# Normalising every softmax tile on VectorE instead of every other one

## The chip, the cores and the metric

The kernel runs on one Trainium2 chip, on all 8 of its cores. Each core has a matmul engine (TensorE, PE in the profile, with PEld for its weight loads), VectorE (DVE), ScalarE (ACT), GpSimd (POOL) and SyncE (SP), and 16 DMA engines. All eight cores run the same program on different data and exchange nothing with one another. The metric is the device time in microseconds (us) of the slowest core. Less is better.

## The reference, cut to what matters

The whole computation is a layer norm, then an attention block and a mixture of experts on the same normalised input, both added to the input:

```python
xn = _layernorm(x, axis=-1)                       # x: (4, 2048, 2048)
x = x + attn(xn, Wqkv, bqkv, Wout, bout) + ffn(xn, gate, gate_up, down, alpha)

# attn: 16 heads of 128, 4 key and value groups
scores = jnp.einsum('bqhd,bkhd->bhqk', q, k) / HD
prob = jax.nn.softmax(scores, axis=-1)
out = jnp.einsum('bhqk,bkhd->bqhd', prob, v).reshape(b, s, D)
return out @ Wout + bout

# ffn: 32 experts, top 8 by softmax of xn @ gate.T; per expert silu(g) * u, then down
```

The change concerns one line of it, the softmax: its last step divides each row of exponentials by the row's sum.

## The kernel before

Core c takes one half (1024 rows) of the sequence of batch c // 2 as its own queries, and keys and values of all 2048 rows. The stages follow one another, with a barrier over PE, DVE and ACT between them: layer norm and transposes, the gate, the projections to q, k and v (L490), attention (here), the output projection (L686), the 32 experts (L828 and L764), and the last transposes with the store (L880, L890).

The order of the work is written out by hand. The Builder class keeps one list of instructions for each engine, and each engine runs its list strictly in order. An operation of VectorE or ScalarE also waits until the one before it on the same engine has finished. What depends on another engine waits for a count: `st` counts PE's batches, `sv` VectorE's operations, `ss` ScalarE's.

The attention stage works on 128 tiles, i = 0 to 127. Tile i is head h = i // 8 and query block q = i % 8: 128 queries against 2048 keys. The steps of one tile are:

- **Scores** (L562): four matmuls of 128x512 into `ps_a`, which is four banks and the only buffer for scores. So the scores of tile i wait until the exponential of tile i-1 has read `ps_a`.
- **Exponential** (L577) on ACT: 128x2048 from `ps_a` to `p_exp0` or `p_exp1` (f32), with the row sum in `ssum2`. Then a logarithm of the sum (L580).
- **Bias and reciprocal** (L583, L585) on DVE: 128x1 each. The bias is what the exponential of tile i+2 subtracts.
- **Norm**: `pn_sb = p_exp * rssum`, 128x2048, f32 to bf16. For even i it runs on DVE (L589), for odd i on ACT (L595).
- **Transposes** (L608) on PE: 16 of 128x128 into `ps_b`. Then a **copy** (L622) on DVE from `ps_b` to `pnT`.
- Once a head (8 tiles) is transposed, **PV** (L636): 32 matmuls of 128x512 into the two halves of `ps_d`, and two copies to `attn_o` on ACT (L645).

The order in which a turn of the loop hands these out is what decides who waits. In turn i, PE gets the scores of tile i, then (if i % 8 is 2 and i is 10 or more) PV of the head before, then the transposes of tile i-2. DVE gets the copy of tile i-2, then bias and reciprocal of tile i, and the norm if i is even. ACT gets the two PV copies where there are any, then the exponential and the logarithm of tile i, and the norm if i is odd. So of the 127 intervals from one exponential to the next, 15 hold a PV (those that end at i = 10, 18, ..., 122), and PV of the last head comes after the loop. An interval that begins at an even tile is called even to odd below, one that begins at an odd tile odd to even.

Of the kernel before, what the change touches and what calls it, by code (L numbers as in the profile page):

```python
# [7 lines left out]
AF = mybir.ActivationFunctionType  # L8
# [94 lines left out]
def build_program():  # L103
# [18 lines left out]
    def sb(name, shape, dtype, off):  # L122
        return nc.alloc_sbuf_tensor_at(name, shape, dtype, offset=MBASE + off).ap()
# [38 lines left out]
    ssum2 = [sm.get("ssum2a", 1), sm.get("ssum2b", 1)]  # L162
    lns2 = [sm.get("lns2a", 1), sm.get("lns2b", 1)]
    nmax2 = [sm.get("nmax2a", 1), sm.get("nmax2b", 1)]
    rssum = sm.get("rssum", 1)
# [64 lines left out]
    p_exp = [sb("p_exp0", [128, S], F32, DYN), sb("p_exp1", [128, S], F32, 65536)]  # L230
    pn_sb = [sb("pn_sb0", [128, S], BF16, 24576), sb("pn_sb1", [128, S], BF16, 61440)]
# [20 lines left out]
    B = Builder(nc)  # L252
# [222 lines left out]
    for jc in range(24):  # L475
# [7 lines left out]
        for tblk in tblks:  # L483
# [22 lines left out]
            if jc < 16:  # L506
# [4 lines left out]
                                 scale=1.0 / HD), "ss")  # L511
# [32 lines left out]
    ev_normC = [None] * 128  # L544
    ev_biasC = [None] * 128
    ev_tpC = {}
# [22 lines left out]
    def emit_softmax(i, ev_sc):  # L569
        qb2 = i % 2  # L570
        B.wait("scalar", "st", ev_sc)
        if i >= 2:
            B.wait("scalar", ev_normC[i - 2][0], ev_normC[i - 2][1])
            B.wait("scalar", "sv", ev_biasC[i - 2])
        else:
            B.wait("scalar", "sv", ev_nz)
        ev_expC[i] = B.op("scalar", lambda e, qb2=qb2: e.activation(  # L577
            p_exp[qb2][:], ps_a[:], AF.Exp, bias=nmax2[qb2][:],
            accum_out=ssum2[qb2][:]), "ss")
        ev_ln = B.op("scalar", lambda e, qb2=qb2: e.activation(  # L580
            lns2[qb2][:], ssum2[qb2][:], AF.Ln), "ss")
        B.wait("vector", "ss", ev_ln)
        ev_biasC[i] = B.op("vector", lambda e, qb2=qb2: e.tensor_tensor(  # L583
            nmax2[qb2][:], nmax2[qb2][:], lns2[qb2][:], ALU.subtract), "sv")
        ev_rc = B.op("vector", lambda e, qb2=qb2: e.reciprocal(rssum[:], ssum2[qb2][:]), "sv")  # L585
        if i % 2 == 0:
            if (i - 2, 1) in ev_tpC:
                B.wait("vector", ev_tpC[(i - 2, 1)][0], ev_tpC[(i - 2, 1)][1])
            ev_normC[i] = ("sv", B.op("vector", lambda e, qb2=qb2: e.tensor_scalar_mul(  # L589
                pn_sb[qb2][:], p_exp[qb2][:], rssum[:]), "sv"))  # L590
        else:
            B.wait("scalar", "sv", ev_rc)
            if (i - 2, 1) in ev_tpC:
                B.wait("scalar", ev_tpC[(i - 2, 1)][0], ev_tpC[(i - 2, 1)][1])
            ev_normC[i] = ("ss", B.op("scalar", lambda e, qb2=qb2: e.activation(  # L595
                pn_sb[qb2][:], p_exp[qb2][:], AF.Identity, scale=rssum[:]), "ss"))

    def emit_tp(i):
        h, q = divmod(i, 8)
# [54 lines left out]
    for i in range(128):  # L654
        ev_sc = emit_scores(i)
        if i >= 2:
            if i % 8 == 2 and i >= 10:
                emit_pv(i // 8 - 1)
            emit_tp(i - 2)
            ev_pv_vlast[0] = B.cnt["sv"]  # L660
        emit_softmax(i, ev_sc)
# [296 lines left out]
```

How the kernel before makes its waits and increments, by code:

```python
    def op(self, eng, fn, inc=None, n=1):  # L43
        auto = self.SELF_SEM.get(eng)
        if auto is not None:
            assert inc in (None, auto), (eng, inc)
            self.wait(eng, auto, self.cnt[auto])
            inc = auto
            n = 1
        if inc is None:
            self.streams[eng].append(lambda e, fn=fn: fn(e))
            return None
        self.cnt[inc] += n
        sem = self.sems[inc]
        self.streams[eng].append(
            lambda e, fn=fn, sem=sem, n=n: fn(e).then_inc(sem, n))
        return self.cnt[inc]
# [4 lines left out]
    def wait(self, eng, semname, val):  # L62
        if val is None or val <= 0:
            return
        self.streams[eng].append(
            lambda e, s=self.sems[semname], v=val: e.wait_ge(s, v))
```

## Time and profile before

| | us |
|---|---|
| median of 3 runs | 5631.75 |
| lowest and highest run | 5631.26 and 5634.69 |
| the profiled execution's own time | 5630.57 |
| span of its slowest core (core 0) | 5629.0 |
| spans of the 8 cores | 5609.8 to 5629.0 |

| engine, whole span of core 0 | busy us | share |
|---|---|---|
| PE | 5033.4 | 89% |
| DVE | 1639.2 | 29% |
| ACT | 875.2 | 16% |
| POOL | 258.4 | 5% |

The span runs from the core's first instruction to its last. The profiled execution's own time is 1.6 us above it. The rows further below are from core 0 where they don't say otherwise. An idle time in square brackets stands in front of the operation that ended it, with the operation that released it. The busy times are those of the whole program, of which attention is about an eighth, so they don't say what bounds that stage. A few per cent of core 0's matmul records are missing: where a batch of four scores shows x3, its first one is not in the trace and its start reads late.

### The profile page before, as it was taken

Reading aid. Unit: us, or ns where it says so; the run is one execution under the profiler, and the core shown is the slowest. Engines: PE = TensorE matmul, PEld = TensorE weight load, DVE = VectorE, ACT = ScalarE, POOL = GpSimd, SP = SyncE. Lnnn points to the kernel's source line nnn. Section 1 sums busy time; section 2 is a strip of 40 time slices with the busy share of each in tenths; the row PEclk is TensorE's granted clock in tenths of the full one; section 3 lists DMA queues with packets and bytes.
Section 4 is the critical chain, followed back from the end, with each engine's and each line's share of the span. In section 5 each row is a group of like instructions: output and inputs, shape, how many; then the busy total and the mean of one; then the engine's idle time right before and its main releaser. Section 6 shows DMA issues by size and latency. Waiting matters only on the chain.

```text
span 5629.0 us, 63025 instructions; the slowest of 8 cores (5609.8 to 5629.0 us)
## 1 busy us (share of the span) xinstructions
PE 5033.4 (89%) x23551; PEld 2390.1 (42%) x24008; DVE 1639.2 (29%) x2416; ACT 875.2 (16%) x1109; POOL 258.4 (5%) x493
## 2 busy tenths in 40 slices
PE   3588656669899999999999999999999999999995
PEld 2434433334444444444444444444444444444443
DVE  3300334330122333322222222333322222223333
ACT  4212666651000000000000000000000000000000
POOL 0000000000000000000000000000000000000000
PEclk9599788869999999999999999999999999999997
DMA  4241000005544434444444444434444444444333
GB/s 167 75 68 23 1 1 1 1 3 83 95 73 74 75 68 74 73 79 72 75 73 74 75 72 75 72 69 78 72 78 73 75 72 74 75 74 73 68 64 120
DMA packets 79879, 378.30 MB, mean 67 GB/s; under 512 B 9696, under 2 KB 10848, under 8 KB 65248
## 3 DMA queue, kind: packets, MB, share of 16 engines
q0 software_dynamic: 70416, 323.03, 32.5%
q1 hardware_dynamic: 9168, 51.21, 2.7%
q8 instruction: 201, 3.29, 0.2%
q14 instruction: 94, 0.77, 0.0%
HBM read 688.80 MB, written 8.39 MB: 124 GB/s over the span
## 4 chain that ended last, share of the span: by engine, by line
PE 85%; ACT 6%; DVE 3%; DMA 3%; issue 2%; DVEq 0%; ACTq 0%; SPq 0%; POOLq 0%
PE ps_a L828 47%; PE ps_d L764 23%; PE ps_a L490 4%; ACT p_exp L577 3%; PE ps_d L636 2%; PE ps_a L562 2%; PE ps_a L686 2%; ACT pn_sb L595 2%; PE ps_b L796 1%; PE ps_b L608 1%; DMA x_re<-x_own 1%; PE ps_b L394 1%; DVE pnT L622 1%; DMA wgubuf<-gu 1%; PE ps_b L353 1%
## 5 line engine op out<-in xcount | busy, mean ns | idle before, releaser
L828 PE MATMUL ps_a<-xn_own,wgubuf 128*128 128x512 bf16 x12044 | 2692.8, 384 | 26.8 <-DMA wgubuf<-gu 12.8
L828 PEld LDWEIGHTS ps_a<-xn_own,wgubuf 128*128 128x128 bf16 x12288 | 1212.0, 99 | 1517.6 <-issue 104.4
L764 PE MATMUL ps_d<-hstash,wdbuf 128*128 128x512 bf16 x6016 | 1330.8, 379 | 10.3
L851 DVE TENSOR_TENSOR sg_sb<-ps_a,sg_sb 128x512 f32<-128x512 f32 x384 | 265.7, 692 | 2407.3 <-PE ps_a L828 2407.3
L764 PEld LDWEIGHTS ps_d<-hstash,wdbuf 128*128 128x128 bf16 x6144 | 595.9, 97 | 741.1 <-issue 181.8
L774 DVE TENSOR_TENSOR ffn_acc<-ffn_acc,ps_d 128x512 f32<-128x512 f32 x1024 | 704.8, 688 | 605.2 <-PE ps_d L764 602.0
L841 ACT ACTIVATE sg_sb<-ps_a 128x512 f32<-128x512 f32 x384 | 229.2, 597 | 2262.7 <-PE ps_a L828 2262.7
L562 PE MATMUL ps_a<-k_sb,q_sb 128*128 128x512 bf16 x470 | 172.9, 502 | 251.6 <-ACT p_exp L577 163.9
L60 POOL DMA_DIRECT2D wgubuf<-gu x384 | 202.6, 528 | 2604.4 <-PE ps_a L828 2555.6
L856 DVE TENSOR_TENSOR hstash<-sg_sb,c_rep 128x512 bf16<-128x512 f32 x384 | 265.9, 693 | 42.3 <-DVE sg_sb L851 3.2
L806 ACT ACTIVATE c_rep<-ps_b 128x512 f32<-128x512 f32 x64 | 38.2, 597 | 1533.0 <-PE ps_b L796 1533.0
L622 DVE COPY pnT<-ps_b 128x2048 bf16<-128x2048 bf16 x128 | 156.7, 1225 | 286.1 <-PE ps_b L608 284.7
L608 PEld LDWEIGHTS ps_b<-ident_b,pn_sb 128*128 128x128 bf16 x2048 | 179.8, 125 | 53.2 <-issue 40.5
L608 PE MATMUL ps_b<-ident_b,pn_sb 128*128 128x128 bf16 x2048 | 192.5, 268 | 3.3 <-ACT pn_sb L595 1.8
L562 PEld LDWEIGHTS ps_a<-k_sb,q_sb 128*128 128x128 bf16 x512 | 48.0, 110 | 314.3 <-issue 298.1
L490 PE MATMUL ps_a<-xn_own,wjbuf 128*128 128x512 bf16 x752 | 168.7, 383 | 8.9 <-DMA wjbuf<-wqkv 7.7
L577 ACT ACTIVATE p_exp<-ps_a,nmax2b 128x2048 f32<-128x2048 f32 x64 | 125.9, 1967 | 105.4 <-PE ps_a L562 105.4
L595 ACT ACTIVATE pn_sb<-p_exp,rssum 128x2048 bf16<-128x2048 f32 x64 | 128.1, 2002 | 69.6 <-DVE rssum L585 62.9
L577 ACT ACTIVATE p_exp<-ps_a,nmax2a 128x2048 f32<-128x2048 f32 x64 | 125.9, 1967 | 12.1 <-PE ps_a L562 5.7
L353 PE MATMUL ps_b<-ident_b,xnbf 128*128 128x128 bf16 x256 | 32.6, 308 | 106.1 <-ACT xnbf L335 82.5
L636 PE MATMUL ps_d<-pnT,vt_sb 128*128 128x512 bf16 x501 | 120.1, 397 | 2.9 <-DVE pnT L622 2.1
L686 PE MATMUL ps_a<-attn_o,woutbuf 128*128 128x512 bf16 x502 | 112.8, 385 | 8.0 <-DMA woutbuf<-wout 7.5
(99 smaller groups left out, 1149.7 us busy)
## 6 DMA issues: line engine op xcount, KB each, us to landing
wgubuf<-gu POOLq DMA_DIRECT2D x384, 512.0 KB, 5.1
wdbuf<-down POOLq DMA_DIRECT2D x64, 1536.0 KB, 10.7
xtile<-x_own SPq DMA_DIRECT2D x16, 1024.0 KB, 5.6
xtile<-x_nbr SPq DMA_DIRECT2D x16, 1024.0 KB, 5.5
wjbuf<-wqkv POOLq DMA_DIRECT2D x24, 512.0 KB, 5.1
woutbuf<-wout POOLq DMA_DIRECT2D x16, 512.0 KB, 5.0
x_re<-x_own SPq DMA_DIRECT2D x8, 1024.0 KB, 7.2
o<-out_sb SPq DMA_DIRECT2D x8, 1024.0 KB, 4.8
```

Source lines behind the costliest of these rows:

```text
L490: ins = e.matmul(ps_a[:, bank * 512:(bank + 1) * 512], wjbuf[jc % 2][:, dc * 128:(dc + 1) * 128], xn_mv(dc, tblk), start=(dc == 0), stop=( ...
L562: ins = e.matmul(ps_a[:, kb * 512:(kb + 1) * 512], q_sb[:, h * TOWN + q * 128: h * TOWN + q * 128 + 128], k_sb[:, g * S + kb * 512: g * S ...
L577: ev_expC[i] = B.op("scalar", lambda e, qb2=qb2: e.activation(p_exp[qb2][:], ps_a[:], AF.Exp, bias=nmax2[qb2][:], accum_out=ssum2[qb2][:]) ...
L595: ev_normC[i] = ("ss", B.op("scalar", lambda e, qb2=qb2: e.activation(pn_sb[qb2][:], p_exp[qb2][:], AF.Identity, scale=rssum[:]), "ss"))
L608: ins = e.matmul(ps_b[:, k * 1024 + j * 128: k * 1024 + (j + 1) * 128], pn_sb[qb2][:, kc * 128:(kc + 1) * 128], ident_b[:], is_transpose=True,
L636: ins = e.matmul(pv_ps, vt_sb[:, (g * 16 + kc) * 128:(g * 16 + kc) * 128 + 128], pnT[:, kc * TOWN + qb * 512: kc * TOWN + qb * 512 + 512], ...
L764: ins = e_.matmul(ps_d[:, slot * 512:(slot + 1) * 512], wdbuf[gh % 3][:, (dc % 8) * 768 + icc * 128: (dc % 8) * 768 + icc * 128 + 128], hs ...
L774: e_.tensor_tensor(ffn_acc[:, dc * TOWN + tb * 512: dc * TOWN + tb * 512 + 512], ffn_acc[:, dc * TOWN + tb * 512: dc * TOWN + tb * 512 + 512],
L828: ins = e_.matmul(ps_a[:, bank * 512:(bank + 1) * 512], wgubuf[bufi][:, dc * 128:(dc + 1) * 128], xn_own[:, dc * TOWN + tb * 512: dc * TOW ...
L841: ev_silu[(e, ip, tb)] = B.op("scalar", lambda e_, tb=tb: e_.activation(sg_sb[:, tb * 512:(tb + 1) * 512], ps_a[:, tb * 512:(tb + 1) * 512 ...
L851: ev_h1[(e, ip, tb)] = B.op("vector", lambda e_, tb=tb: e_.tensor_tensor(sg_sb[:, tb * 512:(tb + 1) * 512], ps_a[:, (2 + tb) * 512:(3 + tb ...
L856: e_.tensor_tensor(hstash[e2 % 2][:, ip * TOWN + tb * 512: ip * TOWN + tb * 512 + 512], sg_sb[:, tb * 512:(tb + 1) * 512], c_rep[e2 % 2][: ...
```

## The change

The norm of odd tiles moves from ACT to DVE, where the norm of even tiles already is. It is the same formula, with the same operands and the other pair of buffers. The wait for the transposes of tile i-2 (they read the same `pn_sb` buffer) moves with it, and the wait of ACT for the reciprocal goes. The event that PE waits for before the transposes of odd tiles is now one of VectorE's.

```diff
-        ev_rc = B.op("vector", lambda e, qb2=qb2: e.reciprocal(rssum[:], ssum2[qb2][:]), "sv")
-        if i % 2 == 0:
-            if (i - 2, 1) in ev_tpC:
-                B.wait("vector", ev_tpC[(i - 2, 1)][0], ev_tpC[(i - 2, 1)][1])
-            ev_normC[i] = ("sv", B.op("vector", lambda e, qb2=qb2: e.tensor_scalar_mul(
-                pn_sb[qb2][:], p_exp[qb2][:], rssum[:]), "sv"))
-        else:
-            B.wait("scalar", "sv", ev_rc)
-            if (i - 2, 1) in ev_tpC:
-                B.wait("scalar", ev_tpC[(i - 2, 1)][0], ev_tpC[(i - 2, 1)][1])
-            ev_normC[i] = ("ss", B.op("scalar", lambda e, qb2=qb2: e.activation(
-                pn_sb[qb2][:], p_exp[qb2][:], AF.Identity, scale=rssum[:]), "ss"))
+        B.op("vector", lambda e, qb2=qb2: e.reciprocal(rssum[:], ssum2[qb2][:]))
+        if (i - 2, 1) in ev_tpC:
+            B.wait("vector", ev_tpC[(i - 2, 1)][0], ev_tpC[(i - 2, 1)][1])
+        ev_normC[i] = ("sv", B.op("vector", lambda e, qb2=qb2: e.tensor_scalar_mul(
+            pn_sb[qb2][:], p_exp[qb2][:], rssum[:]), "sv"))
```

VectorE in the middle of a head, two tiles before the change. `pn_sb_139` and `p_exp_137` are the buffers of even tiles, `pn_sb_140` and `p_exp_138` those of odd ones.

```order
L622 COPY pnT<-ps_b 128x16x128
L583 TENSOR_TENSOR nmax2a<-nmax2a,lns2a 128x1
L585 RECIPROCAL rssum<-ssum2a 128x1
L589 TENSOR_SCALAR pn_sb_139<-p_exp_137,rssum 128x2048
L622 COPY pnT<-ps_b 128x16x128
L583 TENSOR_TENSOR nmax2b<-nmax2b,lns2b 128x1
L585 RECIPROCAL rssum<-ssum2b 128x1
```

The same place with the change, where the lines behind it have moved up by seven.

```order
L615 COPY pnT<-ps_b 128x16x128
L583 TENSOR_TENSOR nmax2a<-nmax2a,lns2a 128x1
L585 RECIPROCAL rssum<-ssum2a 128x1
L588 TENSOR_SCALAR pn_sb_139<-p_exp_137,rssum 128x2048
L615 COPY pnT<-ps_b 128x16x128
L583 TENSOR_TENSOR nmax2b<-nmax2b,lns2b 128x1
L585 RECIPROCAL rssum<-ssum2b 128x1
L588 TENSOR_SCALAR pn_sb_140<-p_exp_138,rssum 128x2048
```

A norm now also stands between the reciprocal of an odd tile and the next copy. ScalarE at the same place and around a PV, before the change:

```order
L577 ACTIVATE p_exp_138,ssum2b<-ps_a,nmax2b 128x2048
L580 ACTIVATE lns2b<-ssum2b 128x1
L595 ACTIVATE pn_sb_140<-p_exp_138,rssum 128x2048
L645 ACTIVATE attn_o<-ps_d 128x512 x2
L577 ACTIVATE p_exp_137,ssum2a<-ps_a,nmax2a 128x2048
L580 ACTIVATE lns2a<-ssum2a 128x1
L577 ACTIVATE p_exp_138,ssum2b<-ps_a,nmax2b 128x2048
L580 ACTIVATE lns2b<-ssum2b 128x1
L595 ACTIVATE pn_sb_140<-p_exp_138,rssum 128x2048
L577 ACTIVATE p_exp_137,ssum2a<-ps_a,nmax2a 128x2048
```

ScalarE there with the change:

```order
L577 ACTIVATE p_exp_138,ssum2b<-ps_a,nmax2b 128x2048
L580 ACTIVATE lns2b<-ssum2b 128x1
L638 ACTIVATE attn_o<-ps_d 128x512 x2
L577 ACTIVATE p_exp_137,ssum2a<-ps_a,nmax2a 128x2048
L580 ACTIVATE lns2a<-ssum2a 128x1
L577 ACTIVATE p_exp_138,ssum2b<-ps_a,nmax2b 128x2048
L580 ACTIVATE lns2b<-ssum2b 128x1
L577 ACTIVATE p_exp_137,ssum2a<-ps_a,nmax2a 128x2048
```

Between the logarithm of an odd tile and the next exponential nothing is left on ACT but the PV copies, once a head. PE's order is the same in both kernels, and so are all DMAs.

## Rows read from the trace of the kernel before

**Rows 1.** Spans and mean granted TensorE clock of the cores.

```profile
core 0: 5629.0 us, clock 0.938
```

**Rows 2.** Busy us (instructions) of PE, PEld, DVE, ACT, POOL; PEclk; DMA; by stretch.

```profile
543.60:1256.00 712.40, 455.66 (x2999) 277.76 (x3053) 280.69 (x450) 435.39 (x478) 0.00 (x0) 0.78 0.00 1
1400.00:5600.00 4200.00, 4094.95 (x18244) 1839.94 (x18613) 1247.91 (x1797) 265.07 (x444) 232.17 (x440) 0.98 0.41 75
```

**Rows 3.** Groups by line: busy us, mean ns | idle before, releasers.

```profile
L562 PE MATMUL ps_a<-k_sb,q_sb 128*128 128x512 bf16 x470 | 172.9, 502 | 251.6 <-ACT p_exp L577 163.9 <-ACT lns2a L580 60.5 <-ACT lns2b L580 24.7
...
L622 DVE COPY pnT<-ps_b 128x2048 bf16<-128x2048 bf16 x128 | 156.7, 1225 | 286.1 <-PE ps_b L608 284.7 <-DVE pn_sb L589 0.3
L595 ACT ACTIVATE pn_sb<-p_exp,rssum 128x2048 bf16<-128x2048 f32 x64 | 128.1, 2002 | 69.6 <-DVE rssum L585 62.9 <-PE ps_a L562 6.7
...
L589 DVE TENSOR_SCALAR pn_sb<-p_exp,rssum 128x2048 bf16<-128x2048 f32 x64 | 82.3, 1287 | 7.3 <-DVE rssum L585 0.7
...
L890 DVE TENSOR_TENSOR out_sb<-ps_a,x_re 128x2048 f32<-128x2048 f32 x8 | 18.3, 2292 | 64.5 <-DMA x_re<-x_own 64.5
```

**Rows 4.** One line, L577: duration ns min/median/max, first and last start.

```profile
L577 ACT ACTIVATE p_exp<-ps_a,nmax2a x64: 1967/1967/1967, 545.7 to 1237.4; 128x2048 f32<-128x2048 f32 x64
...
L577 ACT ACTIVATE p_exp<-ps_a,nmax2b x64: 1967/1967/1968, 550.0 to 1241.5; 128x2048 f32<-128x2048 f32 x64
```

**Rows 5.** Timeline, one pair of tiles: start us, us, operation, [idle before <-releaser].

```profile
708.50 1.97 ACT L577 ACTIVATE p_exp<-ps_a,nmax2a 128x2048 f32<-128x2048 f32 x1
...
710.71 1.86 PE L562 MATMUL ps_a<-k_sb,q_sb 128*128 128x512 bf16 x4 [3.51 <-ACT p_exp L577]
...
712.37 1.90 PE L608 MATMUL ps_b<-ident_b,pn_sb 128*128 128x128 bf16 x16
...
712.84 1.97 ACT L577 ACTIVATE p_exp<-ps_a,nmax2b 128x2048 f32<-128x2048 f32 x1 [1.98 <-PE ps_a L562]
...
715.04 1.02 PE L562 MATMUL ps_a<-k_sb,q_sb 128*128 128x512 bf16 x4 [0.77 <-ACT p_exp L577]
...
716.40 2.00 ACT L595 ACTIVATE pn_sb<-p_exp,rssum 128x2048 bf16<-128x2048 f32 x1 [1.21 <-DVE rssum L585]
...
718.50 1.97 ACT L577 ACTIVATE p_exp<-ps_a,nmax2a 128x2048 f32<-128x2048 f32 x1
```

**Rows 6.** Timeline around a PV.

```profile
722.62 1.97 ACT L577 ACTIVATE p_exp<-ps_a,nmax2b 128x2048 f32<-128x2048 f32 x1 [1.77 <-PE ps_a L562]
...
725.82 7.07 PE L636 MATMUL ps_d<-pnT,vt_sb 128*128 128x512 bf16 x31
...
733.04 0.60 ACT L645 ACTIVATE attn_o<-ps_d 128x512 bf16<-128x512 f32 x1 [2.86 <-PE ps_d L636]
733.73 1.97 ACT L577 ACTIVATE p_exp<-ps_a,nmax2a 128x2048 f32<-128x2048 f32 x1
```

**Rows 7.** Timeline, the tiles right behind that PV.

```profile
735.93 1.02 PE L562 MATMUL ps_a<-k_sb,q_sb 128*128 128x512 bf16 x4 [2.15 <-ACT p_exp L577]
736.25 0.16 DVE L583 TENSOR_TENSOR nmax2a<-nmax2a,lns2a 128x1 f32<-128x1 f32 x1 [1.00 <-ACT lns2a L580]
...
736.79 1.29 DVE L589 TENSOR_SCALAR pn_sb<-p_exp,rssum 128x2048 bf16<-128x2048 f32 x1
736.79 1.06 PE L608 MATMUL ps_b<-ident_b,pn_sb 128*128 128x128 bf16 x16
737.22 1.97 ACT L577 ACTIVATE p_exp<-ps_a,nmax2b 128x2048 f32<-128x2048 f32 x1 [1.14 <-PE ps_a L562]
738.18 1.22 DVE L622 COPY pnT<-ps_b 128x2048 bf16<-128x2048 bf16 x1
...
739.42 1.02 PE L562 MATMUL ps_a<-k_sb,q_sb 128*128 128x512 bf16 x4 [1.57 <-ACT p_exp L577]
```

**Rows 8.** Stretches of that timeline, columns as in rows 2.

```profile
738.00:739.40 1.40, 0.00 (x0) 0.01 (x1) 1.30 (x2) 1.31 (x3) 0.00 (x0) 1.00 0.00 0
...
744.91:748.20 3.29, 3.19 (x19) 2.10 (x18) 1.61 (x3) 1.54 (x1) 0.00 (x0) 0.50 0.00 0
```

## The prediction

> **What bounds the kernel now.** I read the spans first [rows 1]: core 0 is the slowest, and the profiled time is 1.6 us above its span. Then the stages [rows 2]. From 1400 to 5600 us, the experts, PE is busy 4095 of 4200 us at a granted clock of 0.98. The change touches nothing there. In attention, 543.6 to 1256 us, no engine is full: of 712 us PE is busy 456, ACT 435, DVE 281, and PE's clock is 0.78 on average. An unfilled stage like this is bound by a loop of waits, so I went to the groups and then to the timeline. The groups say that PE sat idle 251.6 us before the scores, nearly all of it until ACT had done an exponential or the logarithm just behind it, and that the odd norm (L595) costs ACT 64 x 2002 ns, after another 69.6 us of idling, mostly for DVE's reciprocal [rows 3].
>
> The whole loop runs from exponential to exponential. The first starts at 545.7 and the last at 1241.5 us [rows 4]: 695.8 us for 127 intervals, 15 of them with a PV.
>
> One pair of tiles shows the rhythm [rows 5]. Even to odd: exponential at 708.50, the scores of the next tile released by it at 710.71 (2.21 later), done 1.86 later at 712.57, next exponential 0.27 behind them at 712.84. That is 4.34 us, and only ACT to PE to ACT is in it. Odd to even: 712.84 to 718.50, 5.66 us. Here the scores start at 715.04 and end at 716.06, so the exponential could start at 716.33. But ACT's list has the norm first. It starts only at 716.40, after 1.21 us of waiting for the reciprocal, and ends at 718.40. So the norm holds the loop up for 718.50 - 716.33 = 2.17 us, and PE stands idle meanwhile: the next burst shows the result of it, since the scores at 710.71 had an idle 3.51 us in front of them, took 1.86 us and not 1.02, and the transposes behind them 1.90 us.
>
> **The clock is the second half of the effect.** At the low of its two levels (1.2 GHz, granted 0.50) PE needs 1.86 us for a batch of scores and about 1.90 for the 16 transposes; at the high one (2.4 GHz, granted 1.00) 1.02 and 1.06 [rows 5, 7, 8]. Behind the PV there is a stretch where PE had been busy for 7 us [rows 6] and the idle stretches were shorter: 2.15 us, then 1.57 us. There both score batches took 1.02 us and the clock stayed at 1.00 through the idle from 738.00 to 739.40. The interval 733.73 to 737.22 is 3.49 us [rows 6, 7]. That is the 4.34 of above less 0.84 for the faster scores. The clock fell again before the burst at 744.91 (0.50) [rows 8].
>
> The Trainium skill ("TensorE: Matmul & The Clock Gate", section "HAM oscillation") says that a PE which waits too long between short bursts starts each of them throttled. By that rule, as by my sum, removing the long wait returns the clock; the trace agrees.
>
> **The change, part by part.**
>
> 1. *The norm of odd tiles leaves ACT.* 64 x 2.00 us go. Of these 15 lie beside a PV: from 722.62 to 733.73 us the exponential waits for the PV matmuls (7.07 us from 725.82) and the copy at 733.04 that drains them [rows 6], and 11.11 us stay 11.11. In the other odd intervals what is late next is the scores, at 3.49 us if the clock is up or 4.34 if it is not. One norm lies behind the last exponential.
>
> 2. *The norm of odd tiles comes to DVE.* The even one takes 1287 ns [rows 3]. The odd one I take at the same, since type, shape and operation are the same. Its bounds are 1.29 and the 2.29 of a DVE operation of 128x2048 f32 with two tensor inputs [rows 3]. Does DVE keep up? An even tile's work there runs from 736.25 (bias) over the norm at 736.79 to the end of the copy at 739.40 [rows 7]: 3.15 us, with 0.1 to the next, 3.25. Each tile now has that, against an interval of 3.49. So DVE is a quarter of a microsecond short of being the bound. What is queued behind the odd norm is the copy of the tile before. It waits anyway for transposes that end 1.06 us behind the scores: at 739.42 + 1.02 + 1.06 = 741.5 us by rows 7, when a norm begun at 740.28 (bias 0.54 before it, as at 736.25) would end at 741.57. So the copy is 0.1 to 0.2 us later than before, ends near 742.9, and the next bias is wanted at 740.71 + 2.52 = 743.23. Nobody on the loop waits for it. Cost: nothing, and below zero it can't be, since the only gain of this part is a shorter norm (2.00 - 1.29 = 0.7 us) before the last transposes.
>
> 3. *The waits.* ACT's wait for the reciprocal goes (part of the 2.17). The exponential of tile i+2 now waits for DVE's norm of tile i; that ends 4.35 us after the exponential (738.08 against 733.73) and is wanted two intervals on, at 6.98. Hidden. PE's transposes of an odd tile wait for a norm that ends in front of the next scores' end. Hidden.
>
> 4. *The clock.* With the norm gone PE's longest idle in the loop is that of rows 7, about 1.4 to 1.6 us, in both kinds of intervals, and 2.15 us once behind each PV. Bounds: every interval at 3.49, or every one at 4.34. I take 3.49 for all but the first four, in which PE has few transposes and starts low: 4 x 0.85 = 3.4 us. Because the 2.15 us behind a PV is the stretch with the least work, I allow one interval at 4.34 in 6 of the 15 heads: 5.1 us (0 to 15).
>
> **Sum.** 112 intervals x 3.49 = 390.9; + 3.4 + 5.1; + 15 x 11.11 = 166.7; together 566.1 us in place of 695.8: 129.7 less. With 0.7 at the end 130.4 less. 5630.57 - 130.4 = 5500.2. The median of the runs was 1.2 us above the profiled execution, so 5501 us. All cores run the same loop, so the slowest falls as core 0 does.
>
> **Rivals.**
>
> *A, the clock stays low between PVs.* Then 112 x 4.34 + 166.7 = 652.8, 43 us less: 5588 us. For it: PE has work for 2.1 of 3.49 us only, and long parts of the stage now run low (0.78 on average). Against it: at the low level PE would be working 1.86 + 1.90 of 4.34 us, which is more than in the pairs of rows 5, where the clock came back during one such burst.
>
> *B, the clock goes up and down.* Half of the intervals at 4.34: 56 x 4.34 + 56 x 3.49 + 166.7 = 605.2, 91 less: 5540 us. Against it: two idle stretches of this size in a row (rows 7) did not bring the clock down. The Trainium skill (same page, "A second HAM failure mode: psum-queue depth-cycling") describes just this, a PE that idles briefly but often between groups and whose clock swings. The rows speak for the high level so far, but only for two or three intervals in a row, never for seven.
>
> *C, the odd norm is slower on DVE than the even one.* At 2.29 us DVE's two tiles take 3.25 + 4.25 = 7.5 us against 6.98: 56 x 0.52 = 29 us more than forecast, 5530 us. Against it: same shape, same types, only another buffer. The Trainium skill ("VectorE: DVE Perf Modes", "Mode 2×_2P") gives an f32 operation with one tensor input in SBUF its doubled rate by operand and memory, whichever buffer it is; by that C falls, and no row shows the odd norm.
>
> *D, slower than before.* DVE becomes the bound by contention: norms and copies now fill 2.51 of its 3.25 us a tile, always beside an exponential that writes the same memory. If that stretches them, the interval is 0.74 + 2.51 f. The average interval without a PV was (695.8 - 166.7) / 112 = 4.72, so it decides from f = 1.6. At f = 2 it is 5.76 x 112 + 166.7 = 812, 116 more: 5747 us. Against it: the norm at 736.79 lies for most of its time beside the exponential at 737.22, and the mean of all 64 is 1287 ns too.
>
> *E, nothing gained*, because the exponential waits for something else at the same time: 5632. Against it: rows 5 have the scores ready 2.4 us early.
>
> **How the numbers follow.** Forecast 0.80, A 0.04, B 0.07, C 0.06, D 0.02, E 0.01. A difference under 0.2% (11 us) can't be told from none here. Faster takes the forecast, A, B and C: 0.97; same 0.01; slower 0.02. The forecast alone spans 5489 (no interval low, 8.5 less, and a few us for the clock in the experts' stage) to 5518 (15 heads with one or two low intervals each). To leave no more than 2 in 10 out I take in C and B: 5488 to 5541.
>
> **What would show it.** The first and the last exponential 566 us apart; odd to even equal to even to odd, 3.49 us each, in the middle of a head; 11.1 around a PV; all 128 norms at 1287 ns; a granted clock in the attention stage above 0.95 and the idle before the scores about 1.5 us a tile; ACT's only idle until the scores. The copy should start directly behind the norm, and bias be released by the logarithm. I am wrong if many score batches still take 1.86 us (A, B), if bias waits for the copy of DVE (C, D), or if the experts' stage changes its length by more than a few us.

## The result, and the profile after

| | kernel before | changed kernel |
|---|---|---|
| median of the comparison on record | 6241.73 us (10 runs) | 5683.35 us (8 runs) |
| lowest | 5624.18 us | 5495.42 us |
| ratio to the kernel before | 1 | 0.9766, 95% interval 0.9747 to 0.9785 |
| the same in the later comparison (e9) | 1 | 0.9745, 95% interval 0.9694 to 0.9797 |

In five of the eight runs of the changed kernel the cores of one die had a lower granted clock and took longer (5632 to 6435 us), and the ratio leaves such runs out, as it does six of the ten runs of the kernel before (6126 to 6562 us). The other three runs of the changed kernel took 5495.42, 5499.28 and 5501.25 us. The forecast was 5501 us. The median over all eight, 5683.35 us, lies above its range of 5488 to 5541.

The spans of the first profile show both kinds of cores side by side.

```profile
core 0: 5493.0 us, clock 0.958
...
core 4: 6172.4 us, clock 0.846
```

The stretches, with the columns of [rows 2]. First core 4 of that profile in the experts' stage:

```profile
1400.00:5600.00 4200.00, 4172.54 (x16162) 1732.94 (x16161) 1077.11 (x1562) 232.84 (x390) 205.74 (x390) 0.84 0.35 63
...
3000.00:3400.00 400.00, 397.16 (x1481) 162.25 (x1480) 104.36 (x152) 20.30 (x34) 17.82 (x34) 0.80 0.34 61
```

And core 0 of the same profile at the same time:

```profile
3000.00:3400.00 400.00, 395.01 (x1759) 176.74 (x1794) 122.07 (x177) 25.08 (x42) 22.26 (x42) 0.99 0.41 72
```

Then core 0 of the second profile of the changed kernel (e9), attention and experts:

```profile
543.60:1131.00 587.40, 376.76 (x3088) 227.88 (x3088) 364.26 (x516) 308.66 (x417) 0.00 (x0) 0.95 0.00 1
1400.00:5400.00 4000.00, 3967.07 (x17939) 1764.43 (x17938) 1206.63 (x1750) 254.36 (x426) 223.78 (x424) 0.99 0.42 72
```

Against [rows 2]: the stretch cut out for attention is 587 us long where it was 712, DVE's work in it is up from 281 to 364 us and ACT's down from 435 to 309, and PE's clock is 0.95 in place of 0.78. In the experts' stage core 0 has the clock it had before. Core 4 of the first profile has 0.84, and 0.80 in the middle, where it gets through 1481 matmuls in 400 us and core 0 through 1759.

The groups, answering to [rows 3], of the second profile:

```profile
L588 DVE TENSOR_SCALAR pn_sb<-p_exp,rssum 128x2048 bf16<-128x2048 f32 x128 | 164.7, 1287 | 15.0 <-PE ps_a L562 1.1 <-PE ps_b L601 0.4 <-DVE rssum L585 0.4
L615 DVE COPY pnT<-ps_b 128x2048 bf16<-128x2048 bf16 x128 | 156.7, 1225 | 130.6 <-PE ps_b L601 119.9 <-DVE pn_sb L588 0.5
...
L562 PE MATMUL ps_a<-k_sb,q_sb 128*128 128x512 bf16 x512 | 138.7, 395 | 202.7 <-ACT p_exp L577 201.6 <-DVE vt_sb L539 1.1
```

All 128 norms take 1287 ns on average. PE's idle before the scores is 201.6 us for 127 intervals, 1.59 us each. The loop, answering to [rows 4]:

```profile
L577 ACT ACTIVATE p_exp<-ps_a,nmax2a x64: 1967/1968/1971, 549.0 to 1109.1; 128x2048 f32<-128x2048 f32 x64
...
L577 ACT ACTIVATE p_exp<-ps_a,nmax2b x64: 1967/1967/1969, 553.3 to 1112.6; 128x2048 f32<-128x2048 f32 x64
```

From 549.0 to 1112.6 us it is 563.6 us in place of 695.8; in the first profile it was 567.2 (547.0 to 1114.1). Over the eight cores the mean loop went from 696.0 (690.7 to 703.0) to 565.7 us (563.6 to 568.4) in the second profile. The span fell by 133.5 us from 5629.0 to 5495.5: 132.2 in the loop, 3.3 us were lost before it and 4.6 won behind it.

By kind of interval, on core 0: the 64 even-to-odd ones went from 4.00 to 3.56 us on average, 28 us together; the 48 odd-to-even ones without a PV from 5.54 to 3.56, 95 us; the 15 with a PV, which are all odd to even, from 11.60 to 10.98, 9 us. No even-to-odd interval ever had a norm of ACT in it, so their 28 us are the clock's.

A PV and the tiles behind it, in the same profile:

```profile
690.09 1.97 ACT L577 ACTIVATE p_exp<-ps_a,nmax2b 128x2048 f32<-128x2048 f32 x1 [1.14 <-PE ps_a L562]
...
693.15 7.07 PE L629 MATMUL ps_d<-pnT,vt_sb 128*128 128x512 bf16 x32
...
701.06 1.97 ACT L577 ACTIVATE p_exp<-ps_a,nmax2a 128x2048 f32<-128x2048 f32 x1
...
704.55 1.97 ACT L577 ACTIVATE p_exp<-ps_a,nmax2b 128x2048 f32<-128x2048 f32 x1 [1.14 <-PE ps_a L562]
705.51 1.22 DVE L615 COPY pnT<-ps_b 128x2048 bf16<-128x2048 bf16 x1
...
706.75 1.02 PE L562 MATMUL ps_a<-k_sb,q_sb 128*128 128x512 bf16 x4 [1.57 <-ACT p_exp L577]
707.07 0.16 DVE L583 TENSOR_TENSOR nmax2b<-nmax2b,lns2b 128x1 f32<-128x1 f32 x1 [0.34 <-ACT lns2b L580]
...
707.61 1.29 DVE L588 TENSOR_SCALAR pn_sb<-p_exp,rssum 128x2048 bf16<-128x2048 f32 x1
...
708.04 1.97 ACT L577 ACTIVATE p_exp<-ps_a,nmax2a 128x2048 f32<-128x2048 f32 x1 [1.14 <-PE ps_a L562]
```

Read it against [rows 5] and [rows 6]. 690.09 to 701.06 is 10.97 us, with the PV in it. The interval from the odd tile at 704.55 to the even one at 708.04 is 3.49 us, where it was 5.66. The exponential waits for the scores and for nothing else, the scores take 1.02 us, and bias waits 0.34 us for the logarithm and not for the copy.

### The profile page after: what moved, and what is told of

It reads as the page before. It is cut to its first block, busy times and chain, and to the rows that moved or that the text cites. A ratio compares the mean times of both kernels' runs of the same rounds, so it can differ in the third digit from the quotient of the medians.

```text
span 6172.4 us, 63418 instructions; the slowest of 8 cores (5483.8 to 6172.4 us)
## 1 busy us (share of the span) xinstructions
PE 5656.5 (92%) x24008; PEld 2503.3 (41%) x24008; DVE 1720.4 (28%) x2480; ACT 747.2 (12%) x1045; POOL 258.3 (4%) x493
## 4 chain that ended last, share of the span: by engine, by line
PE 89%; ACT 5%; DMA 3%; DVE 2%; issue 1%; ACTq 0%; DVEq 0%; SPq 0%; POOLq 0%
PE ps_a L821 51%; PE ps_d L757 25%; ACT p_exp L577 4%; PE ps_a L490 3%; PE ps_a L562 2%; PE ps_a L679 2%; PE ps_d L629 2%; PE ps_b L789 1%; DMA x_re<-x_own 1%; PE ps_b L394 1%; DMA wgubuf<-gu 1%; PE ps_b L353 1%; PE ps_d L378 0%; DMA xtile<-x_own 0%; DMA xtile<-x_nbr 0%
## 5 line engine op out<-in xcount | busy, mean ns | idle before, releaser
L821 PE MATMUL ps_a<-xn_own,wgubuf 128*128 128x512 bf16 x12288 | 3144.0, 428 | 11.8 <-DMA wgubuf<-gu 11.8
L821 PEld LDWEIGHTS ps_a<-xn_own,wgubuf 128*128 128x128 bf16 x12288 | 1313.4, 107 | 1858.2 <-issue 1545.0
L757 PE MATMUL ps_d<-hstash,wdbuf 128*128 128x512 bf16 x6144 | 1566.0, 426 | 0.6
L757 PEld LDWEIGHTS ps_d<-hstash,wdbuf 128*128 128x128 bf16 x6144 | 654.1, 107 | 907.2 <-issue 802.3
L562 PE MATMUL ps_a<-k_sb,q_sb 128*128 128x512 bf16 x512 | 141.8, 402 | 199.0 <-ACT p_exp L577 197.9
L588 DVE TENSOR_SCALAR pn_sb<-p_exp,rssum 128x2048 bf16<-128x2048 f32 x128 | 164.6, 1286 | 15.0 <-PE ps_a L562 1.5
L601 PEld LDWEIGHTS ps_b<-ident_b,pn_sb 128*128 128x128 bf16 x2048 | 138.0, 104 | 38.9 <-issue 14.7
L601 PE MATMUL ps_b<-ident_b,pn_sb 128*128 128x128 bf16 x2048 | 149.4, 231 | 4.2 <-DVE pnT L615 4.1
L577 ACT ACTIVATE p_exp<-ps_a,nmax2b 128x2048 f32<-128x2048 f32 x64 | 125.9, 1967 | 77.9 <-PE ps_a L562 68.5
L577 ACT ACTIVATE p_exp<-ps_a,nmax2a 128x2048 f32<-128x2048 f32 x64 | 125.9, 1967 | 66.7 <-PE ps_a L562 57.0
L789 PE MATMUL ps_b<-combineT,selbuf 32*128 32x512 f32 x128 | 88.2, 775 | 34.6 <-ACT c_rep L799 30.5
```

The costliest lines, as they stand in the source:

```text
L562: ins = e.matmul(ps_a[:, kb * 512:(kb + 1) * 512], q_sb[:, h * TOWN + q * 128: h * TOWN + q * 128 + 128], k_sb[:, g * S + kb * 512: g * S ...
L601: ins = e.matmul(ps_b[:, k * 1024 + j * 128: k * 1024 + (j + 1) * 128], pn_sb[qb2][:, kc * 128:(kc + 1) * 128], ident_b[:], is_transpose=True,
L757: ins = e_.matmul(ps_d[:, slot * 512:(slot + 1) * 512], wdbuf[gh % 3][:, (dc % 8) * 768 + icc * 128: (dc % 8) * 768 + icc * 128 + 128], hs ...
L821: ins = e_.matmul(ps_a[:, bank * 512:(bank + 1) * 512], wgubuf[bufi][:, dc * 128:(dc + 1) * 128], xn_own[:, dc * TOWN + tb * 512: dc * TOW ...
```

## The experiments

Times of loops are those of core 0. "Before" in a ratio is always the kernel before on the same chip. The matmuls that e2, e7 and e11 add write to a free half of `ps_d` and nobody reads them. The expectations of e2, e3 and e11 count 56 pairs of intervals without a PV. There are 64 even to odd and 48 odd to even, which makes their loops 644, 623 and 634 us in place of 658, 615 and 625.

**e1, all norms on ACT.**

```diff
-        if i % 2 == 0:
+        if False:
```

> The reverse of the change: the norm of even tiles goes to ACT too, so that all 128 are there. My theory (a norm in ACT's list holds the next exponential up until its end, whatever else is ready): all 112 intervals without a PV become like the odd-to-even ones of the kernel before. From exponential to exponential: 2.35 us to the end of the logarithm, reciprocal ended at 2.95, norm from about 3.15 to 5.15, next exponential at 5.25; with a late copy on DVE up to 5.67. So the loop takes 112 x 5.25 to 5.67 + 15 x 11.0 = 753 to 800 us in place of 696, and the kernel 5690 to 5735 us. Rival 1 (the change gained by the clock alone): PE's idle in even intervals gets longer, at most 4.34 us an interval, so no more than 5632 us. Rival 2 (the norm's own shorter duration on DVE is what counts, 0.7 us each): 64 x 0.7 = 46 us more, 5677 us, with intervals of about 5.

Measured: ratio 1.0141 (1.0112 to 1.017), median of all 4 runs 5708.26 us, loop 768.3 us. A stretch of its timeline:

```profile
702.62 1.97 ACT L577 ACTIVATE p_exp<-ps_a,nmax2b 128x2048 f32<-128x2048 f32 x1
...
704.83 1.86 PE L562 MATMUL ps_a<-k_sb,q_sb 128*128 128x512 bf16 x4 [2.17 <-ACT p_exp L577]
...
705.78 2.00 ACT L595 ACTIVATE pn_sb<-p_exp,rssum 128x2048 bf16<-128x2048 f32 x1 [0.80 <-DVE rssum L585]
...
707.87 1.97 ACT L577 ACTIVATE p_exp<-ps_a,nmax2a 128x2048 f32<-128x2048 f32 x1
```

The scores are ready at 706.69 even at the low clock, and the exponential comes at 707.87, behind the norm: 5.25 us, as expected, and the same number for most intervals of either kind. So a norm on ACT in front of the exponential sets the interval, though the scores are ready. Both rivals had smaller numbers (5632 and 5677 us).

**e2, the kernel before with PE kept busy.**

```diff
+        if i >= 11 and q != 2 and i % 2 == 1:   # in front of the scores
+            6 matmuls 128x512 into ps_d[:, 0:512]
```

> The kernel before, with 6 more matmuls of 128x512 in front of the scores of odd tiles (from the second head on, not behind a PV), whose results nobody uses: they fill part of the 3.5 us in which PE idles there and change nobody's order. It measures the clock's part alone. My theory: the clock stays at its high level, even to odd becomes 3.49 us, odd to even stays at 5.25 us because of the norm on ACT, so the loop takes 56 x 8.74 + 15 x 10.97 + about 4 = 658 us in place of 696 and the kernel about 5594 us (5587 to 5604): the clock is worth about 40 of the 130 us, the wait 90. Rival 1 (the gain was the clock's): the loop comes down most of the way to 566 us, and the kernel to 5520 or less. Rival 2 (the clock is only a by-product and costs nothing in this kernel): 5632 us.

Measured: ratio 0.9948 (0.9924 to 0.9972), median 5597.65 us, loop 666.6 us, granted clock in the loop 0.90:

```profile
543.80:1210.40 666.60, 479.97 (x3347) 271.78 (x3348) 275.71 (x443) 431.31 (x475) 0.00 (x0) 0.90 0.00 1
```

29 us less than 695.8, without any change to who waits for whom, and 23 of them in the even-to-odd intervals (from 4.00 to 3.64 us). The mean over the eight cores went from 696.0 to 664.0. The clock didn't stay up throughout: if it had, the corrected sum of 644 us makes its part 52 us. Odd to even stays at 5.25 us in 27 of 48 intervals. So the clock alone is worth 29 us as measured, 52 by this estimate, and what is left from 644 to 564, about 80 of the 132, needs the norm out of the way.

**e3, the odd norm late on ACT.**

```diff
+        flush()     # behind exponential and logarithm of tile i: norm of tile i-1, if odd
-            ev_normC[i] = ("ss", B.op("scalar", ... pn_sb[qb2], p_exp[qb2], scale=rssum))
+            pend.append((i, ev_rc))   # emitted by the next flush, with scale=rssum1
```

> The kernel before, with the odd norm still on ACT but behind the exponential and logarithm of the next tile, and a reciprocal buffer of its own. It separates where the norm stands from which engine does it. My theory: odd to even falls to 3.49 us as with the change; even to odd now holds exponential, logarithm and the norm, 2.35 + 0.1 + 2.0 + 0.1 = 4.54 us. A pair takes 8.03 us against 8.9 to 10 before and 6.98 with the change: loop 56 x 8.03 + 15 x 11.0 = 615 us, kernel about 5550 us (5540 to 5565). Rival (only taking the work from ACT helps, since ACT is the bound): 5632 us.

Measured: ratio 0.9997 (0.9985 to 1.0009), median 5627.70 us where 5550 was expected, loop 688.8 us. Even to odd took 4.65 us, odd to even 4.21 on average, around a PV 12.6. One pair:

```profile
701.51 1.97 ACT L578 ACTIVATE p_exp<-ps_a,nmax2a 128x2048 f32<-128x2048 f32 x1 [1.74 <-DVE rssum L587]
...
703.71 1.02 PE L563 MATMUL ps_a<-k_sb,q_sb 128*128 128x512 bf16 x4 [1.57 <-ACT p_exp L578]
703.96 2.00 ACT L605 ACTIVATE pn_sb<-p_exp,rssum 128x2048 bf16<-128x2048 f32 x1
...
706.16 1.97 ACT L578 ACTIVATE p_exp<-ps_a,nmax2b 128x2048 f32<-128x2048 f32 x1 [0.20 <-ACT pn_sb L605]
706.21 1.05 PE L618 MATMUL ps_b<-ident_b,pn_sb 128*128 128x128 bf16 x16 [1.48 <-ACT pn_sb L605]
...
708.36 1.87 PE L563 MATMUL ps_a<-k_sb,q_sb 128*128 128x512 bf16 x4 [1.10 <-ACT p_exp L578]
...
710.49 1.97 ACT L578 ACTIVATE p_exp<-ps_a,nmax2a 128x2048 f32<-128x2048 f32 x1 [1.98 <-PE ps_a L563]
```

The scores for the exponential at 706.16 were ready at 704.73; it waited for the late norm. And PE, with the transposes of the odd tile next in its list, now idles 1.48 us for the same norm. The scores at 708.36 run at the low clock. The idle had moved, and hardly shrunk.

**e11, the same with PE kept busy** (5 matmuls of 128x512 in front of the transposes of odd tiles).

```diff
+            emit_keep(i)        # 5 matmuls, odd i only
             emit_tp(i - 2)
```

> The kernel with the odd norm late on ACT, and 5 more matmuls (results unused) in front of the transposes of odd tiles, where PE waits 1.5 us for that norm. It took 4.65 + 4.21 us a pair and 12.6 us around a PV where I had expected 4.54, 3.49 and 11. Theory: half of the scores ran at the low clock, because the late norm moved PE's idle from in front of the scores to in front of the transposes and hardly made it less. With the clock held up a pair takes 4.65 + 3.49 and a PV interval about 11: loop 56 x 8.14 + 165 + 4 = 625 us, kernel 5560 us (5550 to 5575). Rival (the place of the norm brings nothing, on whatever clock): 5620 us.

Measured: ratio 0.9874 (0.9786 to 0.9962), fastest run 5569.26 us, loop 636.1 us at a clock of 0.96. The pair takes 4.65 + 3.58, a PV interval 11.1. So e3's missing gain was the clock's: 688.8 - 636.1 = 53 us. The corrected sum for e11 was 634 us. At nearly the same clock (0.96), e11 against the changed kernel is 636 to 564, and 70 of these 72 us lie in the 64 even-to-odd intervals: 4.65 us on average in place of 3.56, because exponential, logarithm and norm of ACT now fill the interval.

**e4, the PV copies behind the exponential.**

```diff
         emit_softmax(i, ev_sc)
+        if i % 8 == 2 and i >= 10:
+            emit_pvout(i // 8 - 1)     # was part of emit_pv, ahead of emit_softmax
```

> The changed kernel, with ACT's two PV copies behind the exponential of their turn in place of in front of it. My theory: with the norm gone the largest hold-up left in ACT's list is this one. Exponential i starts 3.49 us behind the one before it, beside the PV matmuls. Then PE is the bound: scores end at 3.22, PV 7.07 later at 10.29, transposes at 11.35, scores of tile i+1 at 12.4, exponential i+1 at 12.65 us, where it is 10.97 + 3.49 = 14.46 now. That is 1.8 us x 15 = 27 us less, and the 2.15 us idle behind a PV goes, and with it the low clock there, up to 9 us: kernel 5460 to 5475 us. Rival (DVE, which is 0.24 us a tile short of being the bound, can't catch up with the copy that PV delays, and gives the gain back): 5495 to 5500 us, with bias waiting for the copy in most of the tiles behind a PV.

Measured: fastest of six runs 5454.11 us, no ratio on record. In the profile cores 0 to 3 span 5442.8 to 5453.3 us, where those of the changed kernel's first profile span 5483.8 to 5497.3. Loop 524.0 us, clock 0.99. The two intervals around a PV are 3.49 + 8.66 = 12.15 us in place of 14.46, better than the 12.65 expected, and the low clock behind a PV is gone too. The rival's sign is there and costs nothing:

```profile
652.31 1.22 DVE L615 COPY pnT<-ps_b 128x2048 bf16<-128x2048 bf16 x1 [7.28 <-PE ps_b L601]
...
653.63 0.16 DVE L583 TENSOR_TENSOR nmax2a<-nmax2a,lns2a 128x1 f32<-128x1 f32 x1
...
656.33 1.97 ACT L577 ACTIVATE p_exp<-ps_a,nmax2a 128x2048 f32<-128x2048 f32 x1 [1.14 <-PE ps_a L562]
```

Bias starts right behind the copy, so DVE is behind, yet the exponential is 3.49 us behind the one at 652.84.

**e5, PV spread over the turns.** This is the version that beats both kernels. The two PV copies also move behind the exponential, as in e4.

```diff
         emit_tp(i - 2)
-        if i % 8 == 2 and i >= 10: emit_pv(i // 8 - 1)      # 32 matmuls, ahead of emit_tp
+        j = i - 6                                           # 4 matmuls a turn
+        if j >= 0: emit_pv_part(j // 8, (j % 8) // 4, j % 4)
...
-        if h >= 1 and q == 0: B.wait("vector", "st", ev_pvmm.get((h - 1, 1)))
+        if h >= 1 and q % 4 == 0: B.wait("vector", "st", ev_pvmm[(h - 1, q // 4)])
```

> The changed kernel, with the 32 PV matmuls of a head no longer in one block but four at a time behind the transposes of each turn (first half of the queries from tile 4 of the head on, second half from tile 0 of the next). My theory: with the norm on DVE what is left of the loop is exponential, scores, exponential, 3.49 us, in which PE is idle for 1.3 to 1.4 us. Four PV matmuls take 7.07 / 8 = 0.9 us and fit. So every one of the 127 intervals is 3.49 us, there are none of 11, and PE's clock never falls in the loop: 127 x 3.49 + 4 = 447 us in place of 567, kernel about 5375 us (5365 to 5395). Rival 1: DVE, at 3.25 us a tile, has no PV pause any more in which to catch up, and the PV copies of ACT come on top; the interval settles above 3.6 us and the kernel above 5390. Rival 2: nothing is gained against the block, since PE is the bound: about 5450 us.

Measured: ratio 0.9543 (0.9523 to 0.9564), median 5374.67 us, loop 446.4 us.

```profile
702.89 1.97 ACT L577 ACTIVATE p_exp<-ps_a,nmax2b 128x2048 f32<-128x2048 f32 x1 [1.14 <-PE ps_a L562]
703.36 1.03 PE L631 MATMUL ps_d<-pnT,vt_sb 128*128 128x512 bf16 x4
...
705.09 1.02 PE L562 MATMUL ps_a<-k_sb,q_sb 128*128 128x512 bf16 x4 [0.71 <-ACT p_exp L577]
705.33 0.60 ACT L642 ACTIVATE attn_o<-ps_d 128x512 bf16<-128x512 f32 x1
...
706.38 1.97 ACT L577 ACTIVATE p_exp<-ps_a,nmax2a 128x2048 f32<-128x2048 f32 x1 [0.45 <-PE ps_a L562]
```

PE idles 0.71 us before the scores, the PV copy fits into ACT's idle, and 3.49 us stay 3.49. Against e4, which has the late copies already, spreading alone took the loop from 524.0 to 446.4 us.

**e6, the same with the norm as before** (even on DVE, odd on ACT).

```diff
-            pn_sb[qb2][:], p_exp[qb2][:], rssum[:]), "sv"))     # all tiles on vector
+        (the branch on i % 2 of the kernel before)
```

> The same spread PV, but with the kernel before's norm: even tiles on DVE, odd ones on ACT. Here the clock can't be what differs, since PE gets 3.0 us of work in every interval. My theory: even to odd 3.49, odd to even 5.25 us (norm from 3.15 to 5.15 behind the exponential), both at the high clock: 64 x 3.49 + 63 x 5.25 + 4 = 558 us, 111 us more than with all norms on DVE; kernel about 5486 us (5475 to 5500). Rival (the wait was never worth more than what the clock gave): within 45 us of the kernel with the spread PV and all norms on DVE.

Measured: ratio 0.9894 (0.9851 to 0.9937), fastest run 5570.61 us, loop 644.9 us at a clock of 0.83. That is 85 us more than I expected. Two reasons, both in these rows:

```profile
704.15 1.97 ACT L577 ACTIVATE p_exp<-ps_a,nmax2a 128x2048 f32<-128x2048 f32 x1
...
706.36 1.86 PE L562 MATMUL ps_a<-k_sb,q_sb 128*128 128x512 bf16 x4 [2.68 <-ACT p_exp L577]
...
712.06 2.00 ACT L595 ACTIVATE pn_sb<-p_exp,rssum 128x2048 bf16<-128x2048 f32 x1 [1.23 <-DVE rssum L585]
...
714.16 0.60 ACT L649 ACTIVATE attn_o<-ps_d 128x512 bf16<-128x512 f32 x1
714.85 1.97 ACT L577 ACTIVATE p_exp<-ps_a,nmax2a 128x2048 f32<-128x2048 f32 x1
```

PE still idles 2.68 us in front of these scores and they still take 1.86 us: my premise that PE has enough work here was wrong. And the PV copy now queues behind the norm, in front of the exponential, once every four tiles. The rival fell as well: with PV spread, moving the norm is worth 198 us (644.9 to 446.4). The clock is in that number (0.83 against 0.98): 48 of the 198 us lie in the even-to-odd intervals, which are mostly 4.33 in place of 3.49 us.

**e7, the changed kernel with PE kept busy behind a PV** (6 matmuls of 128x512, in front of the first scores behind it).

```diff
+        if i >= 11 and q == 3:      # in front of the scores
+            6 matmuls 128x512 into ps_d[:, 0:512]
```

> The changed kernel, with 6 more matmuls of 128x512 in front of the first scores behind each PV (results unused), where PE idles 2.15 us. Its 112 intervals without a PV take 400.6 us by the trace of core 0, 112 x 3.49 = 390.9; what lies between, less the 3 us of the start, is what the clock still costs. My theory: the intervals above 3.49 us behind a PV disappear, and the loop falls from 567 to 560 us, the kernel by 5 to 8 us. Rival: those intervals have another cause (DVE behind with its copy) and stay, or grow by the delay that the extra matmuls bring.

(The 112 intervals take 402.6 us by the first profile, 398.9 by the second; the 400.6 in the expectation is a slip.) Measured: loop 558.6 us, clock 0.99, six intervals above 3.55 us where the two profiles of the changed kernel have 18 and 15. Ratio 0.9757 (0.9729 to 0.9786), which can't be told from the changed kernel's own. The loop shows 5 to 9 us on core 0. All eight cores lie at 557.8 to 559.4 us, where those of e9 lie at 563.6 to 568.4, so the loop's gain is shown. The run time alone doesn't settle it.

**e8, more work for DVE in the changed kernel**, and **e10, the same in the kernel with the spread PV.**

```diff
         reciprocal(rssum, ssum2)
+        tensor_tensor(junk, junk, junk, mult)      # 128x256 f32
```

> The changed kernel, with one more operation on DVE behind each reciprocal: 128x256 f32 times itself on a buffer of its own, 0.43 us and 0.1 to the next, so 3.25 becomes 3.78 us of work a tile. It tests how close DVE is to being the bound. Theory 1, my prediction's sum (DVE is the bound as soon as its work exceeds 3.49 us): 112 x 0.29 = 32 us more. Theory 2: a tile's DVE work may lag behind by more than 2 us before PE or ACT has to wait, and each PV block gives it 7 us to catch up, so seven intervals of 0.29 us (2.0 us) are absorbed: 0 to 8 us more.

> The kernel with the spread PV and all norms on DVE, and one more operation of 0.43 us on DVE a tile, as was added to the changed kernel. There is no pause in this loop in which DVE could catch up. Theory (DVE's work a tile is 3.25 us, and the loop takes the larger of that and 3.49): 3.78 us an interval, 127 x 0.29 = 37 us more than the 446 us of the kernel with the spread PV, kernel about 5407 us (5400 to 5415). Rival (bias and copy hand over late as well, so that the waits between PE and DVE add up): 4 us an interval or more, 5435 us or more.

Measured: e8 ratio 0.981 (0.9768 to 0.9852), fastest run 5522.79 us, loop 590.5 us, 23 more than the first profile of the changed kernel and 27 more than the second. e10 ratio 0.9594 (0.9508 to 0.9679), fastest run 5411.12 us, loop 482.9 us, 36.5 more than without. The intervals of these ratios overlap those of the kernels without the extra work (0.9766 and 0.9543); the loops of the eight cores don't: 590.0 to 591.2 against 563.6 to 568.4, 482.1 to 482.9 against 445.6 to 447.2. In e10, 104 of the 127 intervals are 3.78 us, so DVE's sum of 3.25 + 0.53 is the bound as it stands. In e8 the intervals without a PV stay 3.49, and the debt is paid elsewhere:

```profile
652.69 1.97 ACT L579 ACTIVATE p_exp<-ps_a,nmax2b 128x2048 f32<-128x2048 f32 x1 [1.14 <-PE ps_a L564]
...
655.95 1.23 DVE L618 COPY pnT<-ps_b 128x2048 bf16<-128x2048 bf16 x1
...
657.53 7.07 PE L632 MATMUL ps_d<-pnT,vt_sb 128*128 128x512 bf16 x32 [1.62 <-DVE nmax2b L585]
```

The PV needs that copy, which ends at 657.18 (bias, named in the brackets, is only what DVE ended last before it). It starts 4.84 us behind the exponential, where it starts 3.06 behind (693.15 against 690.09) without the extra work. The PV intervals are 13.1 us on average in place of 10.97, 31.8 us together, close to theory 1's 32. The loop grows by less, because the intervals right behind a PV were no longer long: the 112 without a PV take 394.1 us, 8.5 and 4.8 less than in the two profiles without the extra work. Theory 2 had the buffer but had forgotten who waits at its end.

**e9, the changed kernel again.**

> The changed kernel as it is, once more, on the chip and beside the runs that the next two share. Theory: span of core 0 5490 to 5497 us with the loop at 567 us and the granted clock at 0.958, ratio to the kernel before 0.976 to 0.978. Where a die's granted clock in the experts' stage is 0.81 and not 0.98, that die's cores take up to 17% longer there, and that in both kernels alike. Rival (the denser attention stage of the changed kernel has its own effect on the experts' stage): the experts' stage of its cores at 0.98 is longer than the 4241 us of the kernel before's cores by more than 10 us.

Measured: median 5499.66 us of 6 runs, spans 5484.6 to 5496.3 us, loop 563.6 us where 567 was expected, ratio as in the table. From its last output projection to its end core 0 took 4245 us, the kernel before's cores 4237 to 4247. The rival falls.

## Why the prediction was right in its mechanism and wrong in its number

*The step that failed* is the last one of the sum: "The median of the runs was 1.2 us above the profiled execution, so 5501 us. All cores run the same loop, so the slowest falls as core 0 does." It took over the experts' stage as it stood in [rows 2], at a clock of 0.98, for every core and run. In the first profile core 0 did what the sum said (5493.0 us), and core 4 took 679 us more, at 0.84 in that stage: from the last output projection to the end 4924 us against core 0's 4241. The loop wasn't the same for all cores either. On cores 6 and 7 of that profile it took 613.0 and 609.9 us at a clock of 0.77 and 0.78, on the other six 564.2 to 567.1. The sum had no term for any of this, and the range, built only from the unknowns of the change, had no room for it. The prediction did name a longer experts' stage as a sign of being wrong, but gave it no time and no chance. The three runs of the kernel before from which it started (5631 to 5635 us) showed nothing of it; of the next seven, six took 6126 to 6562 us.

What brings a die to that clock, none of these runs shows. The Trainium skill ("TensorE: Matmul & The Clock Gate", section "Seeing it yourself") tells of a peak-current limit that takes a whole die to 13/16 of its clock, 0.81, once three of its cores run dense matmuls. The size fits core 4, the condition doesn't: core 0 stood at 0.99 in the same execution and with the same load on its die. It isn't the change: runs of the kernel before were slow as well. The medians of the two comparisons are 6241.73 and 5734.08 us, and one run of 6193.54 us had cores 0 to 3 at a mean clock of 0.848 and cores 4 to 7 at 0.940 to 0.944.

*The rest, by its own parts*, on core 0 (forecast, first and second profile):

| | forecast | measured |
|---|---|---|
| 112 intervals without a PV | 399.4 us | 402.6 and 398.9 us |
| 15 with a PV | 166.7 us | 164.6 us |
| loop | 566.1 us | 567.2 and 563.6 us |
| from before's 695.8 | -129.7 us | -128.6 and -132.2 us |

The norm leaves ACT: right, and e1 shows it by the opposite. The 2.17 us were those of one pair with the low clock in it; at the high clock the norm holds the loop up for 5.25 - 3.49 = 1.76 us (e2). e3 shows what a sum over ACT's list alone would have missed: whatever waits for the norm must not be next in PE's list. Moving the norm to DVE passed this, since it is done 4.35 us behind the exponential.

The norm comes to DVE: 1287 ns for both kinds, rival C is out. The sum of 3.25 us a tile is confirmed by e10. "Nobody on the loop waits for it" held with 0.24 us to spare, and e8 shows what half a microsecond more would have done, at the PV.

The PV intervals: "11.11 us stay 11.11" was wrong, since it took one block for all. In the kernel before they are 10.97 to 13.42 us, 174.0 together, and with the change all 10.97 or 10.98, 164.6 together. In the block of [rows 6] PV waited for a copy that came late, because the transposes before it ran at the low clock:

```profile
722.15 1.91 PE L608 MATMUL ps_b<-ident_b,pn_sb 128*128 128x128 bf16 x16
...
724.24 1.23 DVE L622 COPY pnT<-ps_b 128x2048 bf16<-128x2048 bf16 x1 [1.40 <-PE ps_b L608]
```

The copy ends at 725.47 and PV starts at 725.82, 3.20 us behind the exponential, where with the change it starts 3.06 behind. In the longest one PV itself took 8.72 in place of 7.07 us. So 9 us of the gain came where the forecast had none. It cost the sum only 2.1 us, because the sum adds up the new loop and not what changes in it.

The clock: it stayed up in the middle of the heads, and behind a PV scores were slow in 8 of 15 heads in both profiles, where I had allowed for 6; that cost about 8 and 6 us where the sum has 5.1. Two or three intervals a profile are 3.77 us long with scores of 1.02 us; their cause is open. Rivals A and B are out. Of the 132 us, e2 measured 29 as the clock's, with the clock at 0.90, and e11 and e3 show 53 us from the clock alone in another order of the same work. The two parts don't simply add: PE idles during the wait, and the scores behind that idle are the slow ones.

## What to carry to other kernels

Where no engine is full, look for the loop of waits and ask for each engine's list what stands in front of the instruction on that loop; an operation of 2 us there cost 1.76 to 2.17 us a turn. Behind that instruction it isn't free either: late on the same engine it cost 1.16 us in the next interval (e11), and moved to an engine with room it cost nothing. Before moving one, ask who waits for it and what that one has next in its own list. And once a loop is set by such waits, its idle time is room: 32 matmuls that cost 7.5 us as a block (5.2 with the copies late, e4) cost nothing four at a time.

## What the runs showed of the hardware

- In one execution of the changed kernel cores 0 to 3 kept a granted clock of 0.99 in the experts' stage. Cores 4 and 5 had 0.99 at first and 0.80 to 0.81 from 2400 us of their spans to the end; cores 6 and 7 had 0.78 to 0.81 from the attention stage up to 4000 us and 0.98 to 0.99 from 4400 us on. From the last output projection to the end core 4 took 16% longer than core 0 (4924 us against 4241).
- With PE idle for 2.15 us and then six times for 1.57 us, once in each interval of 3.49, the granted clock stayed at 1.00 (701.06 to 725.49 us in e9). In 8 of 15 heads of the same profile the idle of 2.15 us behind a PV was followed by slower scores.
- Norms and copies on DVE took 1287 and 1225 ns at 281 us of DVE work in the stage and at 364 us alike. An exponential of ACT overlapped 34 of the 64 norms before and 110 of the 128 with the change (e9), and most of the copies in both.
